# Halo rows by DMA, norms on ScalarE and a freed PSUM bank in an early-fusion kernel

## The reference, cut to what matters

```
for _ in range(10):
    d_down, d_right = differences of u downwards and to the right   # 3x3 taps, zero padded
    q  = max(q - 0.5 * (d_down * vf1 + d_right * vf0), 0)
    Tq = (vf1*q minus its row above) + (vf0*q minus its left column)
    u  = sigmoid((o - Tq) / 0.5)
out = (o - Tq) / 0.5
```

## Time and profile before

| | us |
|---|---|
| median of 3 runs | 1062.35 (1060.9 to 1063.59) |
| profiled execution | 1059.45 |
| its span, first to last instruction | 1057.5 |
| PE busy | 945.2 (89%) |
| DVE busy | 900.7 (85%) |
| ACT busy | 636.8 (60%) |
| POOL busy | 87.9 (8%) |

### The profile page before, as it was taken

One profiled execution on the slowest core, in us unless ns is written; L12 is line 12 of the kernel. 1 busy time (PEld: TensorE's weight loads), 2 busy tenths in 40 slices (PEclk: granted clock), 3 DMA queues, 4 the chain that ended last, 5 costly groups with the idle time before them and its releaser, 6 DMA issues.

```text
span 1057.5 us, 18395 instructions
## 1 busy us (share of the span) xinstructions
PE 945.2 (89%) x6972; PEld 714.7 (68%) x6992; DVE 900.7 (85%) x1318; ACT 636.8 (60%) x2105; POOL 87.9 (8%) x149
## 2 busy tenths in 40 slices
PE   3589999889889989989989988789998999999997
PEld 2367777667667767767767766566666766667675
DVE  4999999999999999999999999798699699543542
ACT  1666667766666666666766665446455564745633
POOL 6100010001010010010010001010000001000000
PEclk9799999999999999999999999999999999999999
DMA  7600000110000110000110000000000000100000
GB/s 162 244 1 2 1 30 6 46 61 1 1 31 11 43 39 21 1 31 11 46 55 2 1 21 2 1 11 2 26 1 26 9 18 1 46 25 2 16 1 30
DMA packets 13544, 28.67 MB, mean 27 GB/s; under 512 B 2704, under 2 KB 9232, under 8 KB 12176
## 3 DMA queue, kind: packets, MB, share of 16 engines
q1 hardware_dynamic: 13072, 26.44, 7.5%
q0 software_dynamic: 384, 1.05, 0.6%
HBM read 22.25 MB, written 5.24 MB: 26 GB/s over the span
## 4 chain that ended last, share of the span: by engine, by line
PE 45%; DVE 43%; ACT 7%; issue 4%; DMA 1%; SPq 0%; POOL 0%; POOLq 0%; ACTq 0%; DVEq 0%
PE ps_t L595 8%; PE ps_t L604 7%; PE ps_s L493 4%; DVE neg_max L1544 4%; PE ps_m L808 3%; PE ps_t L797 3%; DVE f L1538 2%; DVE f L1520 2%; DVE f L1516 2%; DVE f L1519 2%; DVE p L1526 2%; DVE f L1511 2%; DVE p L1523 2%; DVE f L1508 2%; DVE f L1533 2%
## 5 line engine op out<-in xcount | busy, mean ns | idle before, releaser
L1010 ACT ACTIVATE prob<-ps_s,neg_max 128x128 f32<-128x128 f32 x512 | 180.1, 379 | 52.2 <-DVE neg_max L1544 52.2
L595 PE MATMUL ps_t<-hT_f,w 128*128 128x256 f32 x512 | 133.0, 404 | 33.1 <-ACT hT_f L1022 17.2
L595 PEld LDWEIGHTS ps_t<-hT_f,w 128*128 128x128 f32 x512 | 95.3, 196 | 58.9 <-ACT hidT L1076 23.9
L1018 ACT ACTIVATE probT<-ps_t 128x512 f32<-128x512 f32 x128 | 77.2, 603 | 83.2 <-PE ps_t L554 52.6
L604 PE MATMUL ps_t<-w,hidT 128*128 128x256 f32 x512 | 125.4, 383 | 0.0
L1010 ACT ACTIVATION_READ_ACCUMULATOR prob<-ps_s,neg_max 128x1 f32 x512 | 112.8, 220 | 0.0
L604 PEld LDWEIGHTS ps_t<-w,hidT 128*128 128x128 f32 x512 | 91.1, 190 | 12.2 <-issue 3.0
L797 PE MATMUL ps_t<-km,w_fc 128*128 128x384 f32 x256 | 94.4, 504 | 1.7 <-ACT km L1183 1.0
L554 PE MATMUL ps_t<-ident,prob 128*128 128x128 f32 x512 | 81.4, 283 | 5.9 <-ACT prob L1010 3.7
L1076 ACT ACTIVATE hidT<-ps_t,b 128x256 f32<-128x256 f32 x128 | 54.8, 491 | 49.8 <-PE ps_t L595 49.8
L554 PEld LDWEIGHTS ps_t<-ident,prob 128*128 128x128 f32 x512 | 63.0, 145 | 28.4 <-issue 11.8
(11 more groups left out here) (172 smaller groups left out, 1879.3 us busy)
## 6 DMA issues: line engine op xcount, KB each, us to landing
w<-in_w SPq DMA_DIRECT2D x8, 1024.0 KB, 4.9
w_attn<-in_w_attn SPq DMA_DIRECT2D x4, 768.0 KB, 4.6
out<-w SPq DMA_DIRECT2D x7, 384.0 KB, 2.4
o_all<-in_o SPq DMA_DIRECT2D x4, 512.0 KB, 10.5
filtered<-f_out SPq DMA_DIRECT2D x4, 512.0 KB, 2.6
x<-filtered SPq DMA_DIRECT2D x8, 256.0 KB, 2.7
vf<-in_vf SPq DMA_DIRECT2D x4, 256.0 KB
w_attn<-in_w_attn SPq DMA_DIRECT2D x4, 256.0 KB, 3.1
```

The lines of the kernel that those rows point to most:

```text
L595: last = mm(ps_t[:, 0, D * (m % 2):D * (m % 2) + D], w1[:, c, P * m:P * m + P], hT_f[:, c], start=(c == 0), stop=(c == KC - 1))
L1010: last = A(prob[:, n % 2, hh], ps_s[n % 2][:, hh], ACT.Exp, scale=-1.0, bias=neg_max[:, n % 2, hh:hh + 1], accum_out=den)
L1018: A(probT[:, 4 * half:4 * half + 4].rearrange("p h k -> p (h k)"), ps_t[:, 1], ACT.Copy).then_inc(s["act_pT"], 1)
```

## The change

Rows of neighbours: `u` and `p1` get a fifth row. The row below is copied by two transfers of 63 partitions each (one an image) that ScalarE issues right behind its tanh. The row above is copied by two such transfers that SyncE issues when the flux is made. TensorE's halo products go. VectorE's differences and divergence become whole 1024-element operations, in two halves each (`differences_across`, `differences_down`; `divergence_across`, `divergence`).

PSUM: the halo tile's bank becomes `ps_y`. The attention residual, its norm and turn use it, and the pieces of `ff1` alternate between it and `ps_t[:, 0]`.

Norms: GpSimd makes rstd and -mean * rstd; ScalarE applies them (`scaled_rows`, `norm_x`, `norm_y`), except for the first fusion norm of x and the norms of the last layer. `copy_text` for samples 1 to 7 moves to ScalarE; the values' bias is added there as they leave the key product.

SyncE: images and fusion weights are loaded during the text blocks, between the halo transfers. The order on TensorE, ScalarE and VectorE is rewritten throughout.

```diff
@@ ScalarE @@
+            def rows_below(it):
+                act.wait_ge(s["act_tanh"], it + 1)
+                for at in (0, 64):
+                    act.dma_start(u[at:at + 63, RPP, 0:IMG], u[at + 1:at + 64, 0, 0:IMG]).then_inc(s["halo_u"], 16)
             def filter_out(it):
...
-                    A(u[:, :, 0:IMG], fa, ACT.Tanh, scale=0.25).then_inc(s["act_tanh"], 1)
+                    A(u[:, 0:RPP, 0:IMG], fa, ACT.Tanh, scale=0.25).then_inc(s["act_tanh"], 1)
+                    rows_below(it + 1)
@@ SyncE @@
+            def rows_above(it):
+                sp.wait_ge(s["dve_flux"], it + 1)
+                for at in (0, 64):
+                    sp.dma_start(p1[at + 1:at + 64, 0], p1[at:at + 63, RPP]).then_inc(s["halo_p"], 16)
@@ VectorE @@
+            def differences_down(it):
+                dve.wait_ge(s["halo_u"], 32 * it + 32)
+                link(tt(fa, u[:, 1:, 0:IMG], u[:, 0:RPP, 0:IMG], ALU.subtract))
                 link(tt(fa, fa, vf[:, 0], ALU.mult))
             def divergence(it):
-                dve.wait_ge(s["pe_halo"], 2 * it + 2)
-                link(tt(fa[:, 0], p1[:, 0], halo[:, 1], ALU.subtract))
+                dve.wait_ge(s["dve_flux"], it + 1)
+                dve.wait_ge(s["halo_p"], 32 * it + 32)
+                link(tt(fa, p1[:, 1:], p1[:, 0:RPP], ALU.subtract))
                 link(tt(fa, fa, fb, ALU.add))
@@ GpSimd, the other scales alike @@
             def scale_attn(k):
+                pool.tensor_tensor(neg_mean_a[:], mv_a[:, :, 0], minus[:, 0:2], ALU.mult).then_inc(s["pool_eps_a"], 1)
...
+                pool.tensor_tensor(shift_a[:], neg_mean_a[:], rstd_a[:], ALU.mult).then_inc(s["pool_shift_a"], 1)
@@ ScalarE @@
+            def scaled_rows(k, bank, rstd_, shift_):
+                hp = h[:, 2 * (k % PAIRS):2 * (k % PAIRS) + 2]
+                for t in range(2):
+                    last = A(hp[:, t], bank[:, D * t:D * t + D], ACT.Identity, scale=rstd_[:, t:t + 1], bias=shift_[:, t:t + 1])
@@ TensorE @@
             def ff1(k, j):
-                else:
-                    pe_.wait_ge(s["act_ff1"], 4 * k + j)
+                elif j >= 2:
+                    pe_.wait_ge(s["act_ff1"], 4 * k + j - 1)
```

More of the change, by code:

```diff
@@ new lines, in _ @@
+            for k in range(BLOCKS):
+                it, its, l = sum(BLOCK_ITERS[:k]), BLOCK_ITERS[k], k // PAIRS
+                for i in range(its):
+                    rows_above(it + i)
+                    if i == 0 and k < PAIRS - 1:
+                        load_images(k + 1).then_inc(s["l_img_rest"], 16)
+                    if i == 0 and k % PAIRS == PAIRS - 1 and l + 1 < LAYERS:
+                        load_projections(l + 1)
+                    if i == 0 and k % PAIRS == 0 and l:
+                        load_out(l)
+                    if i == 1 and k % PAIRS == 0 and l:
+                        load_ff_in(l)
+                    pair_done(it + i)
+                if its == 1 and k % PAIRS == 0 and l:
+                    load_ff_in(l)
+                if k % PAIRS == 0 and l:
+                    load_ff_out(l)
+                if k in (1, 2, 5):
+                    load_fusion((1, 2, 5).index(k))
+                if k == BLOCKS - 4:
@@ L864, in fuse_step @@
                 ff_in(n - 1, 1)
+                ff_in(n - 1, 2)
+                ff_out(n - 1, 0, range(0, 1))
+                ff_in(n - 1, 3)
                 tile_turn(n, 0, 0)
@@ L963, in fuse_last @@
                 ff_in(f, 2)
+                ff_out(f, 0, range(0, 1))
                 ff_in(f, 3)
@@ new lines, in fuse_step @@
+                tile_probs(n, 1, 1)
+                relu_out(n - 1, 6)
+                tile_exps(n, 2, 1)
+                tile_sink(n, 2)
+                square(n - 1, 5)
+                square(n - 1, 6)
+                relu_out(n - 1, 7)
+                tile_probs(n, 2, 0)
+                square(n - 1, 7)
+                if its > 0:
+                    filter_out(it)
+                tile_probs(n, 2, 1)
+                norm_x(n + 1)
+                o_out(n)
+                x_out(n + 1)
@@ L1582, in scaled_rows, with norm_ffn_last @@
+                moments(rows_of(ps_t[:, 0]), 2, s["dve_stat_f"])
+            def norm_ffn_last(k):
+                dve.wait_ge(s["dve_stat_f"], k + 1)
+                dve.wait_ge(s["pool_rstd_f"], k + 1)
+                hp, rows = h[:, 2 * (k % PAIRS):2 * (k % PAIRS) + 2], rows_of(ps_t[:, 0])
+                scaled = [tick(stt(hp[:, t], rows[:, t], mv[:, t, 0:1], rows_last[:, 0], ALU.subtract, ALU.mult)) for t in range(2)]
                 for t in range(2):
                     dve.wait_ge(s["chain"], scaled[t])
-                    last = stt(hp[:, t], hp[:, t], rstd_[:, t:t + 1], rows_last[:, 1], ALU.mult, ALU.add)
@@ L1600, in block_step @@
-            def block_step(a, f, it):
-                differences(it)
+                    last = stt(hp[:, t], hp[:, t], rstd[:, t:t + 1], rows_last[:, 1], ALU.mult, ALU.add)
+                    tick(last) if t == 0 else last.then_inc(s["h_ready"], 1)
+            def block_step(a, f, it, its):
+                differences_across(it)
                 head_max(a, 0)
                 moments_attn(f)
+                differences_down(it)
+                advance(it)
+                flux_rows(it)
```

773 lines of the change are left out of this document (386 added, 387 removed).

## The result

The changed kernel takes 1149.76 us (median of four runs, 1149.35 to 1150.2), the kernel before 1061.62 us (1060.78 to 1063.59) on the same chip: ratio 1.083, 95% interval 1.081 to 1.085. It is 8% slower, where 1034 us and a gain were forecast.

A forecast was written before the change was run, and what follows sets the result against it. VectorE was taken to bound text and part of fusion, TensorE the rest. Text -16.0 us, fusion -8.9, -1.7 and -2.0, tail +0.8: -27.8 from 1059.45, plus 2.9 offset, 1034 us; range 1010 to 1052.

The forecast's parts named there:

- VectorE's relief: Text blocks: whole filter operations save VectorE 0.40 us per block, and norms moved to ScalarE 1.82 us.
- An issue is 0.43 us: Behind each tanh: a transfer issue on ScalarE takes as long as SyncE's issue row, 0.43 us.
- x: Behind the tanh on ScalarE: time added by two transfer issues, 0.06 + 2 x 0.43, about 0.9 us.
- rival four: SyncE and ScalarE issue against each other: issue 0.8, x 1.7, 0.8 us more per block, 1046 us; 0.19 with rival three.
- I cost this chain at zero: Feed-forward chain in text blocks: GpSimd's scale and shift come some 0.5 us later, covered by earlier moments and alternating banks.
- rival three: Text blocks: ScalarE or the feed-forward chain becomes the limit, 0.8 us lost per block, 1046 us; 0.19 with rival four.
- Late halos: Three waits per text block: neighbour rows forecast hidden, cost zero; as rival, landing at 4.4 us gives about 1098; chance 0.09.
- the 3.05 us of cover: Rows below, second iteration: time from the second issue's start to VectorE's wait, against landings of 1.7 to 2.7 us.
- Fusion steps: After the text: two-iteration steps -8.9 us, one-iteration steps -1.7, three late steps -2.0.
- A sign that I had named: Whole run: TensorE's busy sum falls by about 50 us and ScalarE's rises by about as much.
- text period over 39.5: Text blocks: the forecast counts as wrong if the period exceeds 39.5 us; 38.9 was expected.
- The wait at the first moments: Text block's end: VectorE waits about 1 us for the output projection, 0.85 more than before.

The follow-up runs named there:

- e2: Changed kernel, but SyncE instead of ScalarE issues the transfers of the rows below; 1108.0 us.
- e5: Kernel before with only the neighbour-row transfers added (rows below issued by ScalarE, above by SyncE) and SyncE's loads between them; 1166.2 us.
- e6: Kernel before with only the neighbour-row transfers and SyncE's loads between them, SyncE issuing all transfers but the very first; 1111.0 us.
- e4: Changed kernel with ScalarE scaling the text norms by constants, without waiting for GpSimd, which still computes the same; 1089.3 us.
- e1: Changed kernel with head 1's maximum back in its old place, right behind the first moments; 1111.6 us.
- e9: Changed kernel with one transfer of 127 rows in place of two of 63, on ScalarE and SyncE, the seam between images left out; 1374.0 us.
- e15: Text blocks of e12 followed by the fusion steps of the kernel before, with SyncE's transfers; 1067.0 us.
- e3: Changed kernel with both text norms scaled on VectorE again and head 1's maximum early, GpSimd making only the reciprocal root; 1105.8 us.
- e7: Changed kernel with text norms on VectorE, head 1's maximum early, and SyncE issuing the rows below (all but the first); 1078.1 us.
- e8: Changed kernel with head 1's maximum early and SyncE issuing the rows below (all but the first), norms staying on ScalarE; 1080.9 us.
- e12: Changed kernel with SyncE's issues, head 1's maximum early and the attention norm on VectorE, the feed-forward norm staying on ScalarE; 1076.9 us.
- e10: Changed kernel with eight unread identity matmuls in TensorE's idle stretch ahead of the turn of h in text blocks; 1136.3 us.
- e17: e15 with the flux of each partition's last row made first, in the first iteration of each text block; 1054.9 us.

## Why the prediction was wrong

The steps in the order of the prediction:

- **VectorE's relief was right.** Filter rows and norms were to take 2.22 us per block. VectorE's work per block went from 579.5 / 596 x 39.97 = 38.87 us to 553.5 / 667 x 44.47 = 36.90: 1.97 us. The text blocks of the kernel before, with the columns of the earlier trace rows:

```profile
60.00:656.00 596.00, 546.17 (x3893) 430.11 (x3892) 579.53 (x737) 404.19 (x1485) 45.02 (x77) 0.99 0.06 21
```

- **"An issue is 0.43 us" was too small.** It is 0.74 on ScalarE, x is 1.59. The 0.43 was a load's; the same queue of the kernel before also had issues of 0.57, 0.60 and 0.66 us, which I passed over, and in the changed kernel SyncE's loads at 406 to 408 us still take 0.42 to 0.47. I had the size as rival four at 1046, but for another reason, that the two engines issue against each other; with all of them on SyncE (e2) an issue still takes 0.70. The larger error was to charge it once, at the block's end: e2 gives 3.04 us per block, e5 against e6 2.93, two per iteration and both iterations. In the earlier trace rows ScalarE is busy 26.8 of 40 us, and I read that as room; in its order of work it had none.
- **"I cost this chain at zero" is the step that failed most.** By e4 the wait for the chains costs 3.46 us per block, and the earlier maximum alone gives back 2.45 (e1). Two things were overlooked together: the diff takes head 1's maximum out of the place beside GpSimd's chain, and what follows instead reads two inputs from SBUF. I noted the first for the scores' sake (rival three) and priced it at 0.8 us; the chain's own slowing, from 1.4 us (e9) to 3.7, I did not have. The earlier trace rows were a measurement beside a neighbour that was being moved.
- **Late halos: right for this kernel's text blocks.** VectorE waits 1.7 us in all for the rows above. From the flux's end to the rows' use it takes two issues and 1.6 us, 3.0 us in all (e15), so of the 3.05 us of cover next to nothing was to spare, and the variants that take the maximum back pay 0.7 us per block (e1, e3, e7, e8, e12), the old order 2.6 (e6).
- **Fusion steps: forecast -8.9, -1.7 and -2.0, measured the other way.** Behind the text 20.4 us were lost: about 4 by ScalarE's issues (after against e8), 8.3 by the new orders and norms (e12 against e15), 8.4 by the transfers (e15 against before). VectorE's wait there for the scores of a tile, after and before:

```profile
DVE rmax L1780 <- PE ps_s L795: 44.1, 11, 6.1
```

```profile
DVE rmax L1687 <- PE ps_s L744: 19.8, 10, 5.0
```

  VectorE's busy time there fell from 278 to 258 us, and the wait in these two lines grew by more than that. Which of the new orders costs what was not taken apart.
- **The clock was not in the sum.** From 60 us to the last text block it is 0.90, before 0.99. It is higher where the waits are shorter (0.97 in e7); e10, which raised it and nothing else that I know of, is worth 13.5 us. A sign that I had named failed beside it: TensorE's busy sum was to fall by about 50 us and rose from 945.2 to 962.1, while ScalarE's rose by 62 where about 50 was forecast. In e3, with the clock at 0.98 over the text, TensorE's sum is 927.2.

The sum for a text block, in periods: 44.47 after, 40.11 without issues on ScalarE and with the maximum early (e8), 38.97 with the rows in time and the attention norm on VectorE (e17). A gain of 1 us per block was to be had, but with only half of the text norms moved, and 5.5 us lay between that and the changed kernel. The sign "text period over 39.5" came true. The wait at the first moments came out at 1.2 us per block where about 1 was forecast. Since x in that sum was 0.7 us too small, this agreement is luck. Of the chances, "slower" had only the 0.09 of late halos; it came by rivals three and four, each priced at 12 us.

## What to carry to other kernels

A duration in a trace belongs to its neighbours: before an operation is moved, look what runs beside it on the other engine, above all beside a short chain on GpSimd. An issue of a transfer is work on the engine that issues it, 0.7 us each here, and has to be placed like any other operation; what it needs to start can be computed first. When a move covers one wait, ask which wait it had covered where it stood.

## What the runs showed of the hardware

- GpSimd's root of 128x2 elements: 0.69 us beside a reduction out of PSUM (e1), 0.70 beside an idle VectorE (e9), 1.55 beside operations with two SBUF inputs (after). The chain of four: 1.4 us, 2.3 with the maximum beside it (e1), 3.7.
- One issue of 63 or 127 rows: 0.74 (after) and 0.61 us (e9) on ScalarE, 0.70 (e2) and 0.59 (e9) on SyncE.
- Landing of 63 rows of 1 KB 1.6 us after the issue (e15), of 127 rows 7.6 and 8.6 us (e9).
